# Two half output projections carried into the Runge-Kutta stages, the first drive read from SBUF, and the stage groups written out

## The reference, cut to what matters

```python
# x: (32, 64, 512), cond: (32, 512)
h = GRU(cond, x)                 # over the 64 times; W_ih, W_hh of 512 x 1536
xn = layernorm(h) * gamma
q, k, v = xn @ Wq, xn @ Wkv      # 16 heads of 128, one K and V; rotary; causal softmax
x = x + softmax(q k^T) v @ Wo    # Wo: 2048 x 512
# Runge-Kutta: state q, p of (32, 512), started from cond; drive is x, one row per time
def derivative(q, p, drive):
    dq = q - q**3 / 3 - p + drive + tanh(q) @ coupling.T + bias
    dp = 0.08 * (q + 0.7 - 0.8 * p)
# 64 times: four derivatives (four stages), q and p stepped with DT = 0.01 and clipped at 20
qs = (q after each time)         # (32, 64, 512)
# feed-forward with weights and rows rounded to 8-bit floats
x = x + down(silu(gate(qs)) * up(qs))   # 512 -> 1408 -> 512
```

## Time and profile before

| | |
|---|---|
| runs | 1607.4, 1600.04, 1605.45 us; median 1605.45 |
| profiled execution | 1600.51 us, span 1598.6 us |
| TensorE busy | 1496.3 us, 94% |
| VectorE busy | 1068.1 us, 67% |
| ScalarE, GpSimd busy | 589.1 and 476.6 us, 37% and 30% |
| TensorE clock granted, mean | 0.987 |

### The profile page before, as it was taken

One profiled execution on the slowest core, in us unless ns is written; L12 is line 12 of the kernel. 1 busy time (PEld: TensorE's weight loads), 2 busy tenths in 40 slices (PEclk: granted clock), 3 DMA queues, 4 the chain that ended last, 5 costly groups with the idle time before them and its releaser, 6 DMA issues.

```text
span 1598.6 us, 46459 instructions
## 1 busy us (share of the span) xinstructions
PE 1496.3 (94%) x16660; PEld 929.7 (58%) x16660; DVE 1068.1 (67%) x3437; ACT 589.1 (37%) x1902; POOL 476.6 (30%) x673
## 2 busy tenths in 40 slices
PE   5999999998799999999999998989999999999995
PEld 1333333335675857676676754656666666666662
DVE  1676677775754546455645532578888888988886
ACT  2454454452112020202011011455555555555552
POOL 0212212111220202021120200245566555655650
PEclk9999999998999999999999999999999999999997
DMA  8112112214200000101000005011111111111111
GB/s 309 43 48 52 44 49 63 62 48 163 14 1 14 13 26 0 26 0 26 0 26 7 20 18 208 22 32 29 37 33 38 47 39 33 36 33 36 33 46 39
DMA packets 90911, 72.58 MB, mean 45 GB/s; under 512 B 32609, under 2 KB 82785, under 8 KB 89697
## 3 DMA queue, kind: packets, MB, share of 16 engines
q1 hardware_dynamic: 71056, 59.09, 12.6%
q10 hardware_dynamic: 18032, 6.88, 1.7%
q0 software_dynamic: 1760, 5.77, 1.3%
HBM read 54.77 MB, written 16.94 MB: 45 GB/s over the span
## 4 chain that ended last, share of the span: by engine, by line
PE 69%; DVE 14%; issue 7%; POOL 5%; ACT 3%; DMA 1%; POOLq 0%; DVEq 0%; SPq 0%; ACTq 0%
PE ps L717 14%; PE ps L707 12%; PE ps L635 11%; PE ps L647 11%; PE ps L825 7%; PE ps L752 3%; PE ps L776 3%; DVE mem L1420 2%; POOL mem L583 2%; DVE mem L1369 2%; ACT mem L1063 2%; POOL mem L565 2%; DVE ps L1396 1%; PE ps L815 1%; PE ps L802 1%
## 5 line engine op out<-in xcount | busy, mean ns | idle before, releaser
L825 PE MATMUL ps<-mem 128*32 128x128 f32 x8192 | 277.7, 276 | 35.1 <-ACT mem L1063 23.2
L825 PEld LDWEIGHTS ps<-mem 128*32 128x32 f32 x8192 | 210.5, 110 | 109.3 <-ACT mem L1063 70.4
L552 POOL TENSOR_TENSOR mem<-mem 128x256 f32<-128x256 f32 x128 | 93.0, 727 | 450.0 <-DVE mem L1280 450.0
L717 PE MATMUL ps<-mem 128*128 128x256 f32 x1024 | 222.3, 379 | 0.0
L717 PEld LDWEIGHTS ps<-mem 128*128 128x128 f32 x1024 | 194.0, 190 | 26.0
L707 PE MATMUL ps<-mem 128*128 128x512 f32 x448 | 196.7, 592 | 0.0
L635 PE MATMUL ps<-mem 128*32 128x384 f32 x2048 | 181.3, 496 | 9.6 <-DMA mem<-in_W_ih 5.7
L647 PE MATMUL ps<-mem 128*32 128x384 f32 x2048 | 177.6, 487 | 2.4 <-DVE mem L1200 2.4
L1023 ACT ACTIVATE mem<-mem 128x512 f32<-128x512 f32 x32 | 19.7, 630 | 386.8 <-DVE mem L1312 386.8
L815 PE MATMUL ps<-mem 128*128 128x128 f32 x768 | 136.9, 301 | 10.2 <-DVE ps L1396 8.7
L1063 ACT ACTIVATE mem<-mem 128x64 f32<-128x64 f32 x512 | 109.8, 250 | 92.0 <-DVE mem L1369 85.4
(11 more groups left out here) (146 smaller groups left out, 2184.1 us busy)
## 6 DMA issues: line engine op xcount, KB each, us to landing
mem<-x_scr SPq DMA_DIRECT2D x128, 64.0 KB, 1.9
mem<-in_xT SPq DMA_DIRECT2D x64, 64.0 KB
mem<-in_Wq SPq DMA_DIRECT2D x1, 4096.0 KB, 12.5
mem<-in_Wo SPq DMA_DIRECT2D x1, 4096.0 KB, 15.0
q_scr<-mem SPq DMA_DIRECT2D x64, 64.0 KB, 1.6
mem<-q_scr SPq DMA_DIRECT2D x64, 64.0 KB, 1.9
out<-mem SPq DMA_DIRECT2D x64, 64.0 KB, 1.6
mem<-in_x SPq DMA_DIRECT2D x14, 256.0 KB, 2.7
```

The costliest lines, as they stand in the source:

```text
L552: pool.tensor_tensor(one, one, turned[h % 2].rearrange("p (b t) -> p b t", t=T), ALU.add).then_inc(qr_done, 1)
L717: mm = pe.matmul(ps[:, h % Q_BANKS, 0:BLK], wq[:, c, h * DH:(h + 1) * DH], xnb[:, c, :], start=(c == 0), stop=(c == NC - 1))
L825: mm = pe.matmul(ps[32 * j:32 * j + 32, st % 2, 0:P], thT[:, c, :], ct[:, c, j * P:(j + 1) * P], start=False, stop=(c == NC - 1), skip_gro ...
```

## The change

Three things.

**Two late halves.** The second-to-last block (6) is now split by time like the last one (7). Its first half is projected in `before(0)` and `before(1)` of the last block (`early_out`, 16 heads, bank 6). Of its second half six heads are projected in `before(2)`, one between the turned probabilities and the last values, one behind those; the other eight, and eleven heads of the last block's second half, are cut into quarters of 128 columns and put into stages of groups 0, 1 and 2. The second half of block 6 is kept in `late_ao`, in SBUF where the GRU's states were; ScalarE copies each values tile of blocks 6 and 7 in two instructions, and two residuals are added in groups 1 and 2 (`part_residual`). SP waits for one half of block 6 before it goes on, and loads the second weight matrix after the x rows of the last half.

**The first drive from SBUF.** `drive[0]` gets its rows of the last four batch rows straight from `xres`, two DMAs in SP's queue and two in ScalarE's, beside the write of x1 to DRAM; its other 28 batch rows are read early. The drives of steps 1 to 3 are read from DRAM as before.

**Written-out groups.** TensorE, ScalarE, GpSimd and VectorE run groups 3 to 14 without the hardware loop (SP keeps its own). On TensorE a loop of one pass, whose variable `nought` is 0, stands around all groups, and `nought` is added to the step that the waits of `stage` are computed from. VectorE also moves steps: `t_bits` of the first part from stage 8 to 9, of the second from stage 9 to 11, and the copy to `tsy` from stage 5 of the next group to stage 15, behind L1503.

```diff
-EARLY_HEADS = 6
-LATE_SLOTS = (1, 1, 0, 2)
+LATE_BANK = {6: 7, 7: 2}
+GAP_HEADS = ((0, 6), (6, 7), (7, 8))
+EARLY_HEADS = {6: 8, 7: 5}
+LATE_SLOTS = (3, 2, 1, 4)
+LATE_FREE = [(0, k) for k in range(16)] + [(1, k) for k in range(11)] + [(2, k) for k in (2, 5, 6, 7, 8, 9, 10)]
...
+        def own_drive(j):
+
+            return drive[0][32 * j + B - BLK_B:32 * j + B, :], xres[0:P:HALF_T, 0, j * P:(j + 1) * P]
...
-            last_x1_rows(0)
+            sp.wait_ge(x1_done, PRIMED + PAIRS * (NBLK - 2) + 2)
+            for j in range(NC // 2):
+                sp.dma_start(*own_drive(j)).then_inc(drive_ld[0], 16)
+            half_x1_rows(NBLK - 1, 0, xres[:, 0, :], 2)
             sp.wait_ge(x1_wr, 16 * B)
-            for s in range(4):
+            for s in range(1, 4):
                 sp.dma_start(drive[s], x1_scr[s].rearrange("j b n -> (j b) n")).then_inc(drive_ld[s], 16)
...
                 def before(part):
 
-                    if not first:
+                    if last and part < 2:
+                        early_out(part * HP, (part + 1) * HP)
+                    if last and part == 2:
+                        late_out(6, *GAP_HEADS[0])
+                    if not first and not last:
                         out_proj(blk - 1, part)
...
+                        stage(4 * g + k // 4 + (nought if isinstance(g, int) else 0), k // 4, k % 4)
+                    slot(k, tile)
+                    if isinstance(g, int):
+                        for blk, h, lo, hi in LATE_UNITS.get((g, k), ()):
+                            mm = late_piece(blk, h, lo, hi)
...
-            in_groups(pe, group)
+            late_out(7, 0, EARLY_HEADS[7])
+            with pe.Fori(0, 1) as nought:
+                in_groups(pe, group, loop=False)
...
-                if tile(2) is not None and k == 5:
-                    wait_if(dve, f_ysc, tile(2))
-                    v.did(dve.tensor_copy(tsy, tsx))
...
-                    if k == 8:
+                    if k == 9:
                         t_bits(v, i, 0)
-                    if k == 9:
-                        t_bits(v, i, 1)
                         t_grid(v, 0)
                     if k == 10:
                         t_added(v, 0)
                     if k == 11:
+                        t_bits(v, i, 1)
                         t_grid(v, 1)
```

More of the change, by code:

```diff
@@ L112, in wait_if, with in_groups @@
         eng.wait_ge(sem, value)
-def in_groups(eng, group):
+def in_groups(eng, group, loop=True):
     def tiles(g):
@@ L123, in in_groups @@
         group(g, True, tiles(g))
-    with eng.Fori(LEAD, NTILE - 1) as g:
-        group(g, True, tiles(g))
+    if loop:
+        with eng.Fori(LEAD, NTILE - 1) as g:
+            group(g, True, tiles(g))
+    else:
+        for g in range(LEAD, NTILE - 1):
+            group(g, True, tiles(g))
     for g in range(NTILE - 1, NTILE + LEAD):
@@ L785, in attn_block @@
                 before(2)
-                if last:
-                    before(3)
                 values(0)
                 turned_probs(1)
-                if not last:
-                    before(3)
+                if last:
+                    late_out(6, *GAP_HEADS[1])
+                before(3)
                 values(1)
@@ L899, in group @@
                     pe.wait_ge(ffn_ld, 16 * 6)
+                for k in range(16):
+                    if isinstance(g, int) and (g, k) == (1, 11):
+                        pe.wait_ge(x1_done, PRIMED + PAIRS * NBLK - 1)
+                    if rk:
+                        stage(4 * g + k // 4 + (nought if isinstance(g, int) else 0), k // 4, k % 4)
[3 more added lines that the diff above has]
+                            mm = late_piece(blk, h, lo, hi)
+                            if h == HEADS - 1 and hi == D:
+                                mm.then_inc(wo_mm, 1)
                 if isinstance(g, int) and g == 2:
                     pe.wait_ge(x1_done, PRIMED + PAIRS * NBLK)
[L902 to L910, removed]
             pe.wait_ge(ct_ld, 16 * 4)
@@ L1123, in group @@
                         stage(4 * g + k // 4, k // 4, k % 4)
+                    if isinstance(g, int) and (g, k) == (0, 0):
+                        act.wait_ge(x1_done, PRIMED + PAIRS * (NBLK - 2) + 2)
+                        for j in range(NC // 2, NC):
+                            act.dma_start(*own_drive(j)).then_inc(drive_ld[0], 16)
                     slot(k, tile)
-            in_groups(act, group)
+            in_groups(act, group, loop=False)
         @block.vector
@@ L1341, in attn_block @@
                     norm(blk + 1)
-                if not first:
+                if last:
+                    part_residual(6, xres[:, 0, :], 0)
+                elif not first:
                     residual(blk - 1)
@@ L1512, in slot @@
                             dve.tensor_tensor(ysc, ysc, qt, ALU.add).then_inc(f_out, 1)
+                if tile(1) is not None and k == 15:
+                    if i is not None:
+                        dve.wait_ge(f_ysc, i + 1)
+                    v.did(dve.tensor_copy(tsy, tsx))
             def t_bits(v, i, half):
```

158 lines of the change are left out of this document (89 added, 69 removed).

## The result

The changed kernel takes 1596.94 us (median of 9 runs, 1590.57 to 1599.15) against 1605.02 (9 runs, 1600.04 to 1607.4). The ratio is 0.9949, 95% interval 0.9933 to 0.9965: 8 us faster, where 27 were forecast. The profiled execution took 1590.57 us with a span of 1588.8.

A forecast was written before the change was run, and what follows sets the result against it. Bound by TensorE through attention, then a DMA gap, then the latency of 256 Runge-Kutta stages that no engine fills. -11 (A and B), -4.5 and -8.4 make -23.9 us: profile 1600.5 to 1576.6, median 1578, range 1567 to 1592.

The forecast's parts named there:

- A: End of attention: fewer heads projected before the last block's values, less small costs of single heads and split copies; -8.1 us.
- B: DMA gap between last projection and first stage: SP's new order and first drive from SBUF shorten it; -2.9 us.
- Rival 4: DMA gap: the weights' backlog drains as late behind the last projection as before, gap gain 0, 1581 us; 9%.
- Rival 3: Loop stages 9 and 11: VectorE's moved steps collide with GpSimd, long-stage gain only -1.2 us, 1585 us; 10%.
- C: Stage latency: 64 stages of groups 0 to 2 and 15 gain 0.08 us each from the register wait; -4.5 us.
- rival 2: TensorE's stage waits: no register in effect, all stages 2.21 us, a group 35.4, total -10, 1592 us; 8%.
- D: Long stages of the loop: moved VectorE steps and no loop branch save 0.7 us a group, 12 groups; -8.4 us.
- Case 2: Same as rival 2: no register wait in effect, stages of 2.21 us throughout, 35.4 us a group; 8%.
- Rival 1: Written-out groups: code fetched too slowly, 55 more blocks stopping TensorE 1.1 us each, +60, 1638 us; 5%.

The follow-up runs named there:

- before_swap: The kernel before with only TensorE's two waits ahead of a stage in the other order (tanh first, seed second); 1601.36 us, ratio 0.9983.
- before_dve: The kernel before with only VectorE's two waits ahead of L1420 in the other order (matmuls first, e-buffer second); 1592.00 us, ratio 0.9933.
- tanh_last: The changed kernel with TensorE's two waits ahead of each stage's first matmul in the other order (tanh first, seed second); 1581.57 us, ratio 0.9846.
- te_loop: The changed kernel with TensorE's groups 3 to 14 back in their hardware loop and the one-pass loop removed; 1585.81 us, ratio 0.9877.

## Why the prediction failed

**A was right.** Forecast -8.1, measured -8.3, and the same in every profile: from the first Exp to the end of the last projection it is 44.8 us in the three with the old attention part and 36.5 in the nine with the new.

**B was right in what it rests on, and its size in part by luck.** Forecast -2.9, and -2.9 in this pair of profiles. But the 12.9 us of `before` are the longest of three (11.7 in before_swap, 11.9 in before_dve), and the 10.0 of the changed kernel are at the short end of the eight with the path from SBUF (10.0 to 11.2). By their means B is -1.6, and A and B together are -9.9, forecast -11. What is steady is the time from the last write's landing to the end of the first stage: 4.3 to 4.8 us in all four kernels that read the first drive from DRAM, 2.0 to 2.1 in the eight others. That is the path from SBUF, 2.2 to 2.8 us where the prediction named 1.2, and it carries the whole of B. Part of it is the clock: the 32 matmuls of that stage took 1.9 us in `before` and 1.2 in the changed kernel. The new order on SP gave nothing besides: the write lands 7.3 to 8.1 us behind the projection with the old order, 8.0 to 9.2 with the new.

**Rival 4's condition held, and its B of 0 did not follow.** The scale rows, the last of the weights, land 7.2 us behind the projection, 7.4 before. The forecast had said the same without noticing it, with its writes landed at 975.5 behind a projection that ends at 967.5. Rival 3 did not happen: the moved steps took 0.48 and 0.55 us.

**C failed, at "the register wait is the faster form by 0.08 us, and it is the one thing that `nought` keeps".** Both halves of that sentence are wrong. `nought` keeps nothing, so there is no register wait in the changed kernel, and stages are at 2.21 in all 16 groups. And the register is not what is fast: with constants and the waits in the other order the stages are at 2.13. The rows of the two stages showed the right gap (tanh to matmul, 0.41 against 0.31), but not what stood in it. The list of tanh's line in the queue would have told, and I had not read it: a register instruction in the loop, in groups 0 to 2 a semaphore instruction. I then gave rival 2 8% with "a register is read where the diff says so", which was the diff's word against the fact, written in the same rival, that the value is known.

Under C the prediction also counts 44 stages for the late quarters, where `LATE_FREE` has 34, and puts the two residuals at nothing, of which the second costs 0.34 us. What C itself could give shows in tanh_last, where its condition holds: groups 0 to 2 and 15 take 2.2 us less than before, some 4.0 if the low clock of the first intervals is left out (an estimate from 2.98 and 3.26 us against 2.13, and 2.39 against 2.21 before), forecast 4.5.

**D was right in size and did not show.** Written out, and on stages of 2.13, a group takes 34.58 us (groups 3 to 14 of tanh_last) against 35.31: -0.73, forecast -0.7. The moves are 0.53 of it. In the changed kernel the base of 2.21 covers all of it, as rival 2 said.

**So the outcome is rival 2,** forecast at -10 in the profile and measured -9.9, with its parts off against each other: +3.7 in the stages for the +1 given there, and 2.3 us that the profile was ahead at block 7. Of the 3.7, groups 3 to 14 make 3.1. Case 2 had 16 x 2.21 = 35.4 for a group; every fourth stage takes 2.23 (35.46), and single stages of 2.27 to 2.56 add another 0.11 on average. Three of these (group 6, stage 2; group 9, stage 10; group 11, stage 6) are 0.06 to 0.07 long in tanh_last and te_loop too, and not in the looped kernels; others, as the 2.42 and 2.44 us in groups 4 and 7, stand in the changed kernel alone. They are under 2 us in all, and not followed further.

**The level was off too.** I put the new median 1.4 us above its profile. It is 6.4 above, because the profiled execution was the fastest of the nine: its mean granted clock was 0.988, that of the median run 0.979. The median before stood 4.9 above its profile, so of the 27 us forecast only 23.9 are the terms of the sum, and the rest is a median set against a profile's level. So 1596.94 lies above a range that reached only to case 2's 1592. At the lower end the sum for the range gives 1569 (1600.5 - 27.5 - 4), not 1567.

**Rival 1 did not happen.** The changed kernel fetched 59 blocks in groups 3 to 14 where 55 more were forecast, and TensorE did not stop for them.

How sound the rest of the sum was shows in tanh_last: with step C made true it took 1581.57 us, 24.4 under the kernel before, where the terms made 23.9. So close a match is in part luck. In its profile, from the last block on, it is 21.7 us: 10.1 to the first stage (forecast 11), 11.0 in the stages (12.9) and 0.6 in the tail (nothing).

## What to carry to other kernels

Where an instruction on the critical path needs two semaphores, look up which of them stands on the instruction and which became an instruction of its own. Put the one that ends last on the instruction itself; here, for constants, that is done by writing it first. Before pricing a change in the form of a wait, read the queue's instructions at both places of the trace, since the chain of waits shows their gap but not their cause. And when a saving is found in a latency that repeats, ask of every other engine in the cycle whether it has the same.

## What the runs showed of the hardware

- A semaphore instruction of 51 ns between the event and TensorE's weight load adds 0.08 us to a stage; one of 21 ns ahead of VectorE's L1481 adds up to 0.07 (loop stages of 2.13 go to 2.06 and 2.10). The Trainium skill (Perfetto Trace Analysis, "Identifying Dependency Chains") says that instructions waiting on several engines may have such instructions inserted ahead of them. The trace agrees, and shows what their order is worth: turning it on both engines took stages 0 to 255 from 568.0 to 542.8 us.
- One semaphore instruction with two waits, standing there since before tanh began, let the weight load start 0.04 us sooner (0.33 behind tanh's start) than one with a single wait (0.37). Why stays open.
- A register instruction of 32 ns that carried tanh's wait put the load 0.38 us behind tanh's start, where the wait on the load itself has 0.31 (before_swap).
- `t_bits` over 640 columns took 1.00 us beside GpSimd's L590 and 0.48 one stage later, with GpSimd idle at its start. The Trainium skill (SBUF — State Buffer, "SBUF: two separate sides") has ports that VectorE and GpSimd share as an exclusive lock. The runs show the two durations, not the lock.
- Between TensorE's idle time and the first stages its granted clock was low in some profiles. The window of tanh_last from 980 to 985 us shows 0.51 of full speed, which is the lower of its two levels (1.2 and 2.4 GHz) for nearly all of it, and its first two intervals took 2.98 and 3.26 us. In the 5 us ahead of it (975 to 980) TensorE was busy for 1.62, still at 1.00. The window:

```profile
980.00:985.00 5.00, 3.69 (x38) 2.11 (x37) 1.72 (x8) 1.22 (x6) 0.91 (x2) 0.51 0.14 39
```
